# One written-out order per engine for all eight sequences, and two element-wise steps moved to ScalarE

## The reference

```
x = x + _L0_attn_a_ref(_layernorm(x), ...)     # selective state space block, 512 inner channels, 16 states
x = x + _L0_ffn_ref(_layernorm(x), ...)        # gate and up 256 -> 768, silu(gate) * up, down 768 -> 256
x = x + _L0_attn_b_ref(_layernorm(x), ...)     # receptance, key, value 256 -> 1024, running sums over time
x = x + _L0_ffn_ref(_layernorm(x), ...)        # the same weights again
```

```
xc = silu(conv(xs) + conv_b)                   # 4 taps along the tokens, one channel at a time
dt = softplus(dt @ W_dt + b_dt)
h[t] = exp(dt * A) * h[t-1] + dt * B * xc      # for each of 512 channels x 16 states
y = sum over states of h * C, + D * xc, times silu(z), times W_out

e = exp(clip(-w * t_rem + K));  eu = exp(clip(U + K))
WKV = (shift(cumsum(e * V)) + eu * V) / (shift(cumsum(e)) + eu)
out = (sigmoid(R) * WKV) @ Wo.T + bo
```

## Time and profile before

| | |
|---|---|
| median of 3 runs | 1985.28 us (1977.0 to 1987.1) |
| span of the profiled execution | 1986.3 us; no other time is listed for it |
| DVE busy | 1604.1 us, 81% |
| PE busy | 1504.7 us, 76% |
| POOL busy | 1344.4 us, 68% |
| ACT busy | 1095.9 us, 55%, with 163 table loads of L956 |
| granted PE clock, mean | 0.879 of full |

### The profile page before, as it was taken

One profiled execution on the slowest core, in us unless ns is written; L12 is line 12 of the kernel. 1 busy time (PEld: TensorE's weight loads), 2 busy tenths in 40 slices (PEclk: granted clock), 3 DMA queues, 4 the chain that ended last, 5 costly groups with the idle time before them and its releaser, 6 DMA issues. The chain is left out here.

```text
span 1986.3 us, 18906 instructions
## 1 busy us (share of the span) xinstructions
PE 1504.7 (76%) x4800; PEld 729.0 (37%) x4800; DVE 1604.1 (81%) x2141; ACT 1095.9 (55%) x1613; POOL 1344.4 (68%) x1067
## 2 busy tenths in 40 slices
PE   5062585689787978789778978789776967898968
PEld 2020222245333443435333443335332443455434
DVE  3586878899988998899888998899898898864551
ACT  4354375655676657665676557665764537423431
POOL 0959668866886679867886679767897657531340
PEclk9575687799899988899899988899888979899979
DMA  4543442542336133632335233622334213211200
GB/s 150 186 139 108 146 153 92 171 134 80 121 104 212 52 125 104 219 94 77 126 114 197 68 109 114 216 86 88 131 120 156 83 68 99 80 45 43 77 21 27
DMA packets 167612, 225.19 MB, mean 113 GB/s; under 512 B 13457, under 2 KB 104082, under 8 KB 167506
## 3 DMA queue, kind: packets, MB, share of 16 engines
q1 hardware_dynamic: 167506, 223.99, 34.5%
HBM read 179.90 MB, written 39.85 MB: 111 GB/s over the span
## 5 line engine op out<-in xcount | busy, mean ns | idle before, releaser
L913 POOL TENSOR_TENSOR bu<-rep,bc 128x512 f32<-128x512 f32 x512 | 651.5, 1297 | 132.2 <-PE ps_y L1381 121.3
L1045 ACT ACTIVATE ps_d<-rep,scale_a 128x512 f32<-128x512 f32 x512 | 340.8, 685 | 347.8 <-DVE bu L1211 344.6
L1204 DVE TENSOR_TENSOR_SCAN ps_d<-ps_d,bu 128x512 f32<-128x512 f32 x384 | 459.2, 1217 | 70.1 <-ACT ps_d L1045 41.7
L1330 PE MATMUL ps_r<-xT,wgu 128*128 128x512 f32 x768 | 367.4, 625 | 47.5 <-ACT hf L1068 14.4
L1381 PE MATMUL ps_y<-bu,sel 128*32 128x512 f32 x1024 | 164.6, 720 | 285.1 <-DVE bu L1211 191.9
L930 POOL TENSOR_TENSOR kv<-sums,kv 128x1024 f32<-128x1024 f32 x64 | 150.5, 2351 | 196.6 <-DVE sums L1298 109.2
L1330 PE MATMUL ps_r<-mix,wkv 128*128 128x512 f32 x512 | 240.3, 612 | 25.5 <-ACT kv L1075 10.5
L1211 DVE TENSOR_TENSOR bu<-ps_d,bc 128x512 f32<-128x512 f32 x384 | 256.3, 669 | 0.0
L956 ACT ACT_TABLE_LOAD x163 | 209.1, 1283 | 64.5 <-PE ps_r L1330 29.9
L1330 PEld LDWEIGHTS ps_r<-xT,wgu 128*128 128x128 f32 x768 | 144.9, 197 | 261.3 <-issue 243.0
L1204 DVE TENSOR_TENSOR_SCAN bu<-ps_d,bu 128x512 f32<-128x512 f32 x128 | 154.7, 1209 | 51.6 <-ACT ps_d L1045 39.3
(11 more groups left out here) (98 smaller groups left out, 2078.4 us busy)
## 6 DMA issues: line engine op xcount, KB each, us to landing
rep<-dd_scratch SPq DMA_DIRECT2D x128, 512.0 KB, 4.9
wgu<-gu_scratch SPq DMA_DIRECT2D x96, 256.0 KB, 3.0
dd_scratch<-xs SPq DMA_DIRECT2D x32, 512.0 KB, 3.5
bc<-bc_scratch SPq DMA_DIRECT2D x64, 256.0 KB, 5.0
win<-w_in_dram SPq DMA_DIRECT2D x64, 128.0 KB, 2.2
xc_scratch<-xc SPq DMA_DIRECT2D x32, 256.0 KB, 3.8
sz_scratch<-xin SPq DMA_DIRECT2D x32, 256.0 KB, 3.2
xg<-xc_scratch SPq DMA_DIRECT2D x32, 256.0 KB, 4.4
```

What stands on the lines that cost most here:

```text
L913: pool.tensor_tensor(bu[:, i % BU, :], rep[:, g % REP, 1, :], bc[:, 0, q, :], ALU.mult)\
L1045: act.activation(ps_d[D_BANK[i]][:, :], rep[:, g % REP, 0, :], ACT.Exp, scale=scale_a[:, a, NQ * j + q:NQ * j + q + 1]).then_inc(decay_rea ...
L1204: dve.tensor_tensor_scan(states, d[:, :], bu[:, i % BU, :], 0.0, ALU.mult, ALU.add)\
L1330: last = pe.matmul(dst, lhs, rhs, start=n == 0, stop=n == len(pairs) - 1)
```

## The change

It has three parts.

1. `OPENING`, `LOOP` and `CLOSING` are replaced by `ORDER`, one list per engine over all eight sequences, in which a name stands for its next number (`numbered`). No two turns need to be alike. The banks of `ps_r` are given by one list (`BANKS`), and `FFN_TURNS` says in which order the feed-forward blocks of F and R share their buffers. The waits are the same in kind, with counts made for this order.
2. The chains on DVE are cut into units of one step: `v_tap`, `v_skip` and `v_gate`, `hv_stats`, `hv_aggr`, `hv_eps` (and the same for f and r), `v_den`, `v_newton`, `v_wkv`. Other work can stand between two steps of a chain.
3. ACT makes the convolution's first tap as Identity with scale and bias (`a_tap`, L1027 of the new file) and 1-(1+u) as Identity with scale -1 (end of `a_ln`, L1061). DVE's L1193 and POOL's L893 are gone.

```diff
+def numbered(text):
+
+    seen, out = {}, []
+    for word in text.split():
+        name, _, times = word.partition("*")
+        for _ in range(int(times or 1)):
+            n = seen[name] = seen.get(name, -1) + 1
+            seq, i = n // COUNTS[name], n % COUNTS[name]
+            out.append((seq, name, NUMBERS[name][i] if name in NUMBERS else i))
+    return out
...
+        "v_evsum v_wkv v_esum v_scan fv_up v_hc v_scan v_kd v_hc v_scan*2 fv_up v_hc v_den v_scan v_newton fv_up "
+        "v_hc v_wkv v_ev v_esum v_evsum v_scan*2 v_hc*2 v_wo v_den v_kd v_newton v_scan v_wkv v_scan fv_up v_hc "
...
-            run(OPENING[letter])
-            for t in range(3, NSEQ):
-                run([(t, unit, i) for unit, i in LOOP[letter]])
-            run(CLOSING[letter])
+            run(order(letter))
...
+                    elif unit == "a_tap":
+                        prev = before(m)
+                        if i == 0 and prev is not None:
+                            act.wait_ge(xc_stored.sem, at(xc_stored, prev, xc_stored.per))
+                            act.wait_ge(dtx_ready.sem, at(dtx_ready, prev, JD))
+                        act.wait_ge(xs_ready.sem, at(xs_ready, m, i + 1))
+                        act.activation(xc[:, i, :], xs[:, i, 0:T], ACT.Identity, bias=col("conv_b", i),
+                                       scale=col("conv_w", TAPS * i)).then_inc(first_tap.sem, 1)
...
                         if i:
                             act.wait_ge(dt_ready.sem, at(dt_ready, m, i))
+                        else:
+                            act.wait_ge(m_full.sem, FULL[m, "p_in", 2 * JD - 1])
                         act.activation(rest_u, dd_slot(i)[:, 1, :], ACT.Identity, bias=ones[:, 0:1]).then_inc(sp_u.sem, 1)
                         act.wait_ge(sp_u.sem, at(sp_u, m, i + 1))
                         need("natural_log_exp_and_others")
                         act.activation(lnu, rest_u, ACT.Ln).then_inc(sp_ln.sem, 1)
+                        act.wait_ge(sp_ln.sem, at(sp_ln, m, i + 1))
+                        act.activation(rest_u, rest_u, ACT.Identity, bias=ones[:, 0:1], scale=-1.0).then_inc(sp_neg.sem, 1)
...
+                    elif unit == "v_tap":
+                        j, tap = i // TAPS, i % TAPS
+                        if tap == 1:
+                            dve.wait_ge(first_tap.sem, at(first_tap, m, j + 1))
+                        else:
+                            dve.wait_ge(conv_tap.sem, at(conv_tap, m, TAP_DONE[i - 1]))
+                        dve.scalar_tensor_tensor(xc[:, j, :], xs[:, j, tap:tap + T], col("conv_w", i), xc[:, j, :],
+                                                 ALU.mult, ALU.add).then_inc(conv_tap.sem, 1)
...
+                    elif unit == "v_den":
+                        den, rec = kv[:, row(i, "eu"), :], ps_r[BANK[r, "a_rec", i]]
                         dve.wait_ge(rec_ready.sem, at(rec_ready, r, i + 1))
-                        dve.tensor_tensor(den, den, rec[:, :], ALU.mult).then_inc(newton.sem, 1)
-                        dve.wait_ge(newton.sem, at(newton, r, 2 * i + 1))
+                        dve.tensor_tensor(den, den, rec[:, :], ALU.mult).then_inc(den_ready.sem, 1)
+                    elif unit == "v_newton":
```

More of the change, by code:

```diff
@@ L425, in full_counts @@
-def full_counts(stage, parts):
-    uses = [(parts.get(u, u), i) for u, i in LOOP["p"] if STAGE[u] == stage and u != "p_y" and u not in parts.values()]
-    return {use: n + 1 for n, use in enumerate(uses)}
-M_FULL = full_counts("H", {})
-F_FULL = full_counts("F", {"fp_turn2": "fp_turn", "fp_down2": "fp_down"})
-K_FULL = full_counts("K", {"p_wo2": "p_wo"})
-R_FULL = full_counts("R", {"rp_turn2": "rp_turn", "rp_down2": "rp_down"})
-BANK = {use: k for k, uses in enumerate(LOOP_BANKS) for use in uses}
+TAP_ORDER = tuple(TAPS * (2 * pair + half) + tap for pair in range(JD // 2) for tap in range(1, TAPS) for half in range(2))
@@ new lines @@
+NUMBERS = {"v_mix": (1, 2, 0), "v_tap": TAP_ORDER, "v_hc": tuple(i for i in range(STEPS) if not by_pool(i)),
+           "g_hc": tuple(i for i in range(STEPS) if by_pool(i))}
+STAGE = {"hp_turn": "H", "p_in": "H", "p_xproj": "H", "p_dt": "H", "p_post": "F", "fp_turn": "F", "fp_gate": "F",
+         "fp_up": "F", "fp_down": "F", "p_recept": "F", "p_k": "K", "p_v": "K", "p_wo": "K", "rp_turn": "R",
+         "rp_gate": "R", "rp_up": "R", "rp_down": "R"}
+SECOND = {"fp_turn2": "fp_turn", "fp_down2": "fp_down", "p_wo2": "p_wo", "rp_turn2": "rp_turn", "rp_down2": "rp_down"}
@@ new lines, with order, full_counts @@
+BANKS = (
[55 rows of a table added]
+)
+FFN_TURNS = [("f", 0), ("f", 1), ("r", 0), ("f", 2), ("r", 1), ("f", 3), ("r", 2), ("f", 4), ("r", 3), ("f", 5),
+              ("r", 4), ("f", 6), ("r", 5), ("f", 7), ("r", 6), ("r", 7)]
+def order(letter):
+    return numbered(ORDER[letter])
+def full_counts():
+    counts, n = {}, dict.fromkeys("HFKR", 0)
+    for seq, unit, i in order("p"):
+        if unit == "p_y" or unit in SECOND.values():
+            continue
+        use = SECOND.get(unit, unit)
+        n[STAGE[use]] += 1
+        counts[seq, use, i] = n[STAGE[use]]
+    return counts
@@ L438 @@
+FULL = full_counts()
+TAKEN = numbered(" ".join(word.split(":")[0] for word in BANKS.split()))
+BANK = {use: int(word.split(":")[1]) for use, word in zip(TAKEN, BANKS.split())}
+USES = [[use for use in TAKEN if BANK[use] == k] for k in range(max(BANK.values(), default=0) + 1)]
+HELD_BEFORE = {use: uses[n - 1] for uses in USES for n, use in enumerate(uses) if n}
+NORMS = {"h": 1, "f": 2, "r": 1}
 class Signal:
@@ L1152, in shifts, with full @@
                                          ALU.mult, ALU.mult).then_inc(n_shift[f].sem, 1)
-            def full(what, seq, counts, unit, i):
-                dve.wait_ge(what.sem, at(what, seq, counts[unit, i]))
-                return ps_r[BANK[unit, i]]
+            def full(what, seq, unit, i):
+                dve.wait_ge(what.sem, FULL[seq, unit, i])
+                return ps_r[BANK[seq, unit, i]]
             def scale_weights():
@@ L1287, in run @@
                     elif unit == "v_esum":
-                        if i:
+                        if i or before(r) is not None:
                             dve.wait_ge(dn_ready.sem, at(dn_ready, r, i))
```

601 lines of the change are left out of this document (418 added, 183 removed), and 343 rows, old and new, of tables (BANKS, CLOSING, CLOSING_BANKS, LOOP).

## The result

The changed kernel takes **1876.17 us** (median of 4 runs, 1873.11 to 1877.58) against 1981.71 us for the kernel before beside it: a ratio of **0.946** (95% interval 0.943 to 0.949). The forecast was 1932 us with a range from 1885 to 1980 us. Three of the kernels further down (decay_ahead, two_ahead, ev_psum) had one execution each in a slower state, which the ratios leave out and which moves their medians by 0.6 us at most; decay_ahead's trace is of such a one and is not read here.

What follows compares the result with a forecast made beforehand. The prediction took DVE to pace the kernel's middle, and PE the rest behind sequence 7. From 1986.3 us its terms, - 53.7 + 8 + 4 - 12, gave 1932.6, stated as 1932 us, range 1885 to 1980.

Steps and rivals of the forecast that it cites:

- term 3: ACT's added taps, negations and table loads, 82 us: scans' waits for decays grow by a tenth, +8 us.
- term 4: Opening: more work ahead of the first g_dt, but the first scan needs three instead of four; +4 us.
- term 5: Sequence 7: a free order brings DVE's idle time from 34 us to the loop's 22; -12 us.
- Terms 1 and 2: DVE sheds 32 first taps at 0.58 us and 294 links (waits between dependent steps) at 0.12 us; -53.7 us.
- Term 6: POOL's negation leaves an engine with time to spare, and SP's queue moves the same transfers: nothing.
- Term 7: Tail behind the last gate: the same matmuls remain, PE's 204.5 us stay; 0, ends -15 and +10.
- A: The free order closes DVE's gaps too, idle time in a turn from 22 to 13 us; 1880 us, chance 0.17.
- B: Links on DVE are worth nothing once other work stands between the steps; 1967 us, chance 0.10.
- C: A chain through several engines, not DVE's sum, sets a turn; 1975 to 1980 us, chance 0.11.
- D: ACT becomes the pace, its whole 82 us delaying scans, and the kernel slower; 2019 us, chance 0.10.

Runs made afterwards that it cites:

- decay_ahead: The kernel before with decay 33 moved ahead of the third a_dt and a_ln in ScalarE's loop; 1973.87 us, ratio 0.995.
- two_ahead: decay_ahead with a second swap in ScalarE's loop, decay 53 ahead of the four a_recept; 1992.19 us, ratio 1.005 to the kernel before.
- ev_psum: The change with 32 of the 64 running sums of e*v reading their product from PSUM, 32 instructions more; 1876.88 us, ratio 0.945.
- early4: The change with sequence 0's softplus sums and first taps on VectorE, some transfers earlier, its first 4 recurrence steps ahead of sequence 1's parts; 1884.85 us, ratio 0.949.
- neg_back: The change with the negation back on GpSimd instead of ScalarE; 1883.30 us, ratio 0.950.
- glue_all: The change with VectorE's chains whole again in the new order, 352 links instead of 32; 1925.65 us, ratio 0.973.

## Why the prediction was wrong

**The step that failed.** Ahead of its terms the sum took it that the new order keeps the loop's 22 us of idle time in a turn. With terms 3, 4 and 5 (+8, +4, -12) DVE's idle time up to the last gate was thus forecast to stay as it is; it fell by 129.7 us, and a turn has 3.5 to 8.4 us now. The second error has the other sign: DVE's busy time was to fall by 53.7 us there and rose by 32.8, since no term stood for GpSimd's products beside it. With the -18.1 us behind the last gate, forecast at 0, these are the 61 us between the 53.7 of the forecast and the 115.0 of the two traces. That the miss is not larger is luck, as the two errors partly cancelled.

**What bounds the kernel.** Right: DVE paces the middle, and now it does so nearly without a gap.

**Terms 1 and 2, the saved work (-53.7).** Right as work, as far as the runs can tell: 0.124 us a link in isolation, and 52 us less of busy time beside the lengthening. (32 x 0.58 us is 18.6, not 18.4.) Its price in time is the order's: in the old one the taps and the negation returned 9 us and single steps cost 87, in the new one the taps return 11 and the steps at most 49.5. The Trainium skill says that the semaphore between two VectorE instructions costs nothing extra (VectorE: DVE Perf Modes, The DRAIN you can't avoid). That does not hold here: eight chained taps took 0.87 us longer than eight unchained. The same section also says that a next instruction that is not held starts earlier, which the prediction left out.

**Term 3, ScalarE's added work (+8).** The size of the work was exact (1178.2 us). "I let these waits grow as ACT's share does" failed: they fell from 81 to 12 us. The order that adds the work also places the decays. With an order that is fixed, 46 us more cost 12.6, all of it before 600 us, so a tenth was also too little there.

**Term 4, the opening (+4).** The first scan was forecast at about 78 us and came at 78.94. But the stretch ended 10.0 us earlier, not later: I priced its first 78 us and left out the 140 behind. These were 154.1 us before and are 139.6 now, with 9.0 us of idle time on DVE instead of 28.6. early4 shows the same from the other side, as the first scan does not set the gate.

**Term 5, sequence 7 (-12, ends 0 and -22).** It was -36.0. The bound "a free order should reach the loop's figure" of 22 us idle was the error: DVE is idle for 7.7 us of that stretch.

**Term 6, GpSimd's negation and SP's queue (0).** neg_back measures 7 us. The reason given, GpSimd's spare time, does not make the work free. The 7 us are waiting, as DVE's busy time does not rise, and they are spread over small waits; which chain makes them stays open. No run tests SP's queue.

**Term 7, the rest (0, ends -15 and +10).** -18.1, just outside. PE's busy time there fell from 204.5 to 200.9 us at a slightly higher clock, and its idle time from 43.9 to 29.4: the longest wait was 13.6 us for a K result before, and is 5.4 us after. That is not tested; glue_all loses only 2 us there.

**The missing term.** None of mine was for DVE beside GpSimd, and in busy time it is larger than any: +94 us. In the kernel before GpSimd waited for the running sums and so mostly stood still beside them. Counted in the two timelines, 50 of the 64 sums at L1292 and 42 of those at L1298 had GpSimd idle for nine tenths of their time or more (all at 1.19 to 1.23 us); after, it is 20 and 14. GpSimd's group that needs the sums, before:

```profile
L930 POOL TENSOR_TENSOR kv<-sums,kv 128x1024 f32<-128x1024 f32 x64 | 150.5, 2351 | 196.6 <-DVE sums L1298 109.2 <-DVE sums L1292 87.0
```

And after:

```profile
L949 POOL TENSOR_TENSOR kv<-sums,kv 128x1024 f32<-128x1024 f32 x64 | 150.8, 2357 | 77.4 <-DVE sums L1345 45.3 <-DVE sums L1351 31.5
```

The order closed many gaps of both engines, and in busy time this has its price. What it costs in time no run shows: ev_psum took 15 us of it out and was no faster. The earlier trace rows carried the hint: `g_bu` in threes takes 1.23 us each, while its mean over the kernel is 1.30 (1297 ns at L913).

**The rivals.** A gave 1880 us and is nearest, for half the reason: it took 9 us of idle time from a turn, while 12 to 18 went and DVE's longer instructions took some back. That it comes within 4 us is luck. B's sign, a busy time that falls by less than 25 us, came true for another reason, the lengthening; B itself fell, as links are worth 0.12 to 0.16 us. C fell, as turns shrank to 209 to 217 us (its own time also counts ScalarE's 8 us twice: 1932 + 38 is 1970). D fell: with 46 us more on ScalarE the loss is 12.6. What failed in the sum had been named as a possibility, which is A, and given 0.17.

**Not tested: PE's clock.** The mean granted clock rose from 0.879 to 0.904 of full, and DVE's waits for the projections ahead of the FFN product fell from 74.6 to 36.1 us. How much of the gain is the clock's, no run separates. In glue_all's four runs the one at 0.857 took 1939.15 us and those at 0.897 to 0.901 took 1924.8 to 1926.4; by that, 0.025 of clock is some 9 us, an estimate.
